# Lower-threshold compare of every second weight piece on GpSimd, in the first ternary feed-forward block

## Chip, cores and metric

One core of one Trainium2 chip. The metric is the device time of the whole kernel in microseconds, lower is better. Engine names are those of the profile: PE is TensorE's matmuls, PEld its weight loads, DVE is VectorE, ACT is ScalarE, POOL is GpSimd, SP is SyncE, which here issues the DMAs.

## What is computed

A macaron layer on x of 4 x 512 tokens by 512 features: half of a feed-forward block, a recurrent attention block, and half of the same feed-forward block again. The change is in the first feed-forward block:

```python
def _quantize(w):
    gamma = jnp.mean(jnp.abs(w))
    return jnp.clip(jnp.round(w / (gamma + EPS)), -1.0, 1.0)

def _bitlinear(x, w):
    return jnp.matmul(x, _quantize(w).T)
x1 = _bitlinear(x, w1)      # w1, w2: 1408 x 512
x2 = _bitlinear(x, w2)
hidden = jax.nn.sigmoid(x1) * x2
return _bitlinear(hidden, w3)   # w3: 512 x 1408

x = x + 0.5 * _L0_ffn_ref(_layernorm(x, axis=-1), L0_ffn_w1, L0_ffn_w2, L0_ffn_w3)
```

A quantised weight is 1 where w is above half of gamma, -1 where it is below minus half of gamma, and 0 between: two comparisons and a subtraction.

## The kernel before, in words

The kernel has three phases, one after the other: `ffn_phase` with `first=True`, the attention, and `ffn_phase` with `first=False`. The first phase quantises the three weights and saves them; the last one loads them. Each engine runs its own list of instructions in the order in which it is written, and waits on semaphores where it needs another's result.

In the first phase, each weight lies in SBUF as 128 partitions by 5632 float32 values, cut into four pieces (k = 0 to 3) of 1408. SP loads the tokens and then the twelve pieces. ACT sums the absolute values of each piece as it lands (L208). PE adds them over the partitions (`total`, L326), and DVE makes the two thresholds `thr` and `nthr` of weight i (`threshold`, L257 to L264). Then `quantise(i)` goes over the four pieces on DVE, two instructions for each:

```python
dve.wait_ge(quantised, KT * i + k)
nc.vector.tensor_scalar(below[:, :], raw[i][:, piece], nthr[:, i:i + 1], None, ALU.is_lt).then_inc(below_ready, 1)
dve.wait_ge(below_ready, KT * i + k + 1)
nc.vector.scalar_tensor_tensor(wq[i][:, piece], raw[i][:, piece], thr[:, i:i + 1],
                               below[:, :], ALU.is_gt, ALU.subtract).then_inc(quantised, 1)
```

The first (L273) writes "below the lower threshold" as bfloat16 into `below`; the second (L276), called the quantising instruction here, compares the piece with the upper threshold and subtracts `below`. There is one buffer `below`, so DVE goes through compare, quantise, compare, quantise, twelve times in all. For w3, `raw[2]` is a part of `x_sb`.

DVE's list in this phase is: norm of the first 512 tokens, their split, threshold and quantise of w1, of w2, of w3, then `hidden(0, 0)` (L284 to L291), which multiplies the two up projections and splits the product into `g_hi` and `g_lo`. PE's list is: transposes, the totals of w1 and w2, the first two row tiles of the w1 product (as each piece is quantised), the total of w3, the same two tiles of w2, then `down_tile(0, 0)` (L379), which needs `g_lo` of `hidden(0, 0)`. From there on PE alternates up tiles and down tiles. SP waits until all twelve pieces are quantised before it loads the other token rows into `x_sb` and saves `wq`. POOL has little to do: the constants, and for each block b of 512 tokens two small instructions on a 128 x 4 tile that make `rstd` (L193, L195), those for b = 1 when DVE has the statistics of the second 512 tokens.

Of the kernel before, what the change touches and what calls it, by code (L numbers as in the profile page):

```python
# [25 lines left out]
BF16 = mybir.dt.bfloat16  # L26
# [4 lines left out]
P = 128  # L31
NB, T, HID = 4, 512, 512
NH = 16
FF = 1408
C = T // P
KT = HID // P
# [10 lines left out]
def ffn_phase(nc, first, x_in, x_out, w_t, wq_dram):  # L47

    with ExitStack() as ctx:  # L49
        def sb(name, shape, dt=FP32):  # L50
            return ctx.enter_context(nc.sbuf_tensor(f"{name}_{int(first)}", shape, dt))

        def sem(name):
            return ctx.enter_context(nc.semaphore(f"{name}_{int(first)}"))
# [18 lines left out]
        hid = sb("hid", [P, 2, T])  # L73
        g_hi = [sb(f"g_hi{i}", [P, T], F32R) for i in range(2)]
        g_lo = [sb(f"g_lo{i}", [P, T], F32R) for i in range(2)]
        if first:
            raw = [sb(f"raw{i}", [P, KT * FF])[:, :] for i in range(2)]
            raw.append(x_sb[:, C:, :].rearrange("p c d -> p (c d)")[:, 0:KT * FF])
            below = sb("below", [P, FF], BF16)
            junk = sb("junk", [P, 3 * HID], BF16)  # L80
            asum = sb("asum", [P, 3, KT])
            tot = sb("tot", [P, 3])
            gamma = sb("gamma", [P, 3])
            thr = sb("thr", [P, 3])
            nthr = sb("nthr", [P, 3])
# [6 lines left out]
        abs_summed = sem("abs_summed")  # L92
        total_ready = sem("total_ready")
        thr_step = sem("thr_step")
        below_ready = sem("below_ready")
        quantised = sem("quantised")
        wq_saved = sem("wq_saved")
        groups = [(m, min(m + 3, MT)) for m in range(0, MT, 3)]
# [83 lines left out]
        @block.gpsimd  # L182
        def _(pool):
            nc.gpsimd.memset(ident[:, :], 0.0).then_inc(consts_ready, 1)
            nc.gpsimd.memset(ones[:, :], 1.0).then_inc(consts_ready, 1)
            nc.gpsimd.memset(eps_t[:, :], LN_EPS).then_inc(consts_ready, 1)
            nc.gpsimd.memset(mhalf[:, :], -0.5).then_inc(consts_ready, 1)
            pool.wait_ge(consts_ready, 4)
            nc.gpsimd.affine_select(out=ident[:, :], in_=ident[:, :], compare_op=ALU.not_equal, fill=1.0, base=0,
                                    pattern=[[-1, P]], channel_multiplier=1).then_inc(consts_ready, 1)  # L190
            for b in range(NB):
                pool.wait_ge(stats_step, 2 * C * (b + 1))
                nc.gpsimd.tensor_tensor(ve[:, :], mv[:, :, 1], eps_t[:, :], ALU.add).then_inc(rstd_step, 1)  # L193
                pool.wait_ge(rstd_step, 2 * b + 1)
                nc.gpsimd.tensor_tensor(rstd[:, :], ve[:, :], mhalf[:, :], ALU.pow).then_inc(rstd_step, 1)  # L195
# [24 lines left out]
        @block.vector  # L220
        def _(dve):
            def x_rows(b, c):
                return x_sb[:, b * C + c, :]

            def norm_stats(b):

                dve.wait_ge(x_full[b], 16)
                nc.vector.memset(gate[:, :], 0.0)
                for c in range(C):
                    nc.vector.bn_stats(stats[:, c, :], x_rows(b, c)).then_inc(stats_step, 1)  # L230
                dve.wait_ge(stats_step, 2 * C * b + C)
                nc.vector.memset(gate[:, :], 0.0)
                for c in range(C):
                    nc.vector.bn_aggr(mv[:, c, :], stats[:, c, :]).then_inc(stats_step, 1)  # L234

            def norm_apply(b):
                dve.wait_ge(rstd_step, 2 * b + 2)
                dve.wait_ge(ln_transposed, KT * b)
                for c in range(C):
                    nc.vector.tensor_scalar(xn[:, c, :], x_rows(b, c), mv[:, c, 0:1], rstd[:, c:c + 1],  # L240
                                            ALU.subtract, ALU.mult).then_inc(xn_ready, 1)

            def split_norm(b, half):

                for k in (2 * half, 2 * half + 1):
                    bank = up_ps[k % 2][pair["rows", b, half]]
                    dve.wait_ge(ln_transposed, KT * b + k + 1)
                    nc.vector.tensor_copy(h_hi[b % 2][:, k, :], bank[:, :]).then_inc(h_split, 1)  # L248
                    dve.wait_ge(h_split, 2 * (KT * b + k) + 1)
                    nc.vector.tensor_tensor(h_lo[b % 2][:, k, :], bank[:, :], h_hi[b % 2][:, k, :].bitcast(FP32),  # L250
                                            ALU.subtract).then_inc(h_split, 1)

            def threshold(i):

                s = 4 * i
                dve.wait_ge(total_ready, i + 1)
                nc.vector.tensor_reduce(tot[:, i:i + 1], out_ps[i][:, 0:KT], AX.X, ALU.add).then_inc(thr_step, 1)  # L257
                dve.wait_ge(thr_step, s + 1)
                nc.vector.tensor_scalar(gamma[:, i:i + 1], tot[:, i:i + 1], 1.0 / (FF * HID), Q_EPS,
                                        ALU.mult, ALU.add).then_inc(thr_step, 1)  # L260
                dve.wait_ge(thr_step, s + 2)
                nc.vector.tensor_scalar(nthr[:, i:i + 1], gamma[:, i:i + 1], -0.5, None,
                                        ALU.mult).then_inc(thr_step, 1)
                nc.vector.tensor_scalar(thr[:, i:i + 1], gamma[:, i:i + 1], 0.5, None,  # L264
                                        ALU.mult).then_inc(thr_step, 1)
                dve.wait_ge(thr_step, s + 4)

            def quantise(i):

                for k in range(KT):  # L270
                    piece = slice(k * FF, (k + 1) * FF)
                    dve.wait_ge(quantised, KT * i + k)
                    nc.vector.tensor_scalar(below[:, :], raw[i][:, piece], nthr[:, i:i + 1], None,  # L273
                                            ALU.is_lt).then_inc(below_ready, 1)
                    dve.wait_ge(below_ready, KT * i + k + 1)
                    nc.vector.scalar_tensor_tensor(wq[i][:, piece], raw[i][:, piece], thr[:, i:i + 1],  # L276
                                                   below[:, :], ALU.is_gt, ALU.subtract).then_inc(quantised, 1)

            def hidden(b, m):

                n = MT * b + m
                dve.wait_ge(sig_ready, n + 1)
                dve.wait_ge(value_in, n + 1)
                nc.vector.tensor_tensor(hid[:, n % 2, :], up_ps[1][pair["tile", b, m]][:, :], sig[:, n % 2, :],  # L284
                                        ALU.mult).then_inc(hid_step, 1)
                dve.wait_ge(hid_step, 3 * n + 1)
                if n >= 2:
                    dve.wait_ge(down_done, n - 1)
                nc.vector.tensor_copy(g_hi[n % 2][:, :], hid[:, n % 2, :]).then_inc(hid_step, 1)  # L289
                dve.wait_ge(hid_step, 3 * n + 2)  # L290
                nc.vector.tensor_tensor(g_lo[n % 2][:, :], hid[:, n % 2, :], g_hi[n % 2][:, :].bitcast(FP32),  # L291
                                        ALU.subtract).then_inc(hid_step, 1)

            def add_output(b):
                dve.wait_ge(down_done, MT * (b + 1))
                for c in range(C):
                    nc.vector.scalar_tensor_tensor(x_rows(b, c), out_ps[c][:, :], 0.5, x_rows(b, c),  # L297
                                                   ALU.mult, ALU.add).then_inc(out_added, 1)

            norm_stats(0)  # L300
            norm_apply(0)
            split_norm(0, 0)
            split_norm(0, 1)
            if first:
                for i in range(3):
                    threshold(i)
                    quantise(i)
            for b in range(NB):
                for m in range(MT):
                    hidden(b, m)  # L310
                    if m == 0 and b > 0:
                        add_output(b - 1)
                    if b + 1 < NB:
                        if m == MT - 7:
                            norm_stats(b + 1)
                        if m == MT - 6:
                            norm_apply(b + 1)
                        if m >= MT - 4 and m < MT - 2:
                            split_norm(b + 1, m - (MT - 4))
            add_output(NB - 1)  # L320
# [1214 lines left out]
```

## Time and profile before

| | us |
|---|---|
| time, median of 3 runs | 3064.88 (3059.52 to 3068.61) |
| the profiled execution | 3062.89 |
| its span in the trace | 3061.2 |
| busy in the span: PE, DVE, ACT, POOL | 2937.7, 2183.8, 1625.3, 1349.5 |

The span is the time from the first instruction of the program to the last, and the execution's own time lies 1.7 us over it. Busy time is the time in which an engine had an instruction of the program under way. The first feed-forward phase takes about the first tenth of the span, the attention about eight tenths.

### The profile page before, as it was taken

What the parts mean: (1) busy time and instruction counts of PE and PEld (TensorE: products, weight loads), DVE (VectorE), ACT (ScalarE), POOL (GpSimd) and SP (SyncE); (2) the same over time, 40 slices, a digit from 0 to 9 for tenths busy, and PEclk for the clock granted to TensorE, in tenths of its full rate; (3) what the DMA queues carried; (4) which work ended last, traced back from release to release, by engine and by line L of the source; (5) the groups of instructions that cost most, each with busy time, mean ns of one, the idle gap of its engine ahead of it and who ended that gap; (6) DMA issues with size and microseconds to landing.
All of it is one profiled execution on the core that took longest, in us unless ns stands there. A gap on an engine that the chain in (4) does not pass through costs nothing. (4 is left out here: it accounts for less than half of the span.)

```text
span 3061.2 us, 44753 instructions
## 1 busy us (share of the span) xinstructions
PE 2937.7 (96%) x14918; PEld 2068.1 (68%) x14918; DVE 2183.8 (71%) x4724; ACT 1625.3 (53%) x3682; POOL 1349.5 (44%) x1999
## 2 busy tenths in 40 slices
PE   5999699999999999999999999999999999996999
PEld 4887466666666666666666666666666666664887
DVE  6553488787785887877868777777678777773553
ACT  3110376666665666666656666666666666660110
POOL 0000465555554555555545555555455555550000
PEclk8999899999999999999999999999999999998999
DMA  6100311111111111111011111110111111105000
GB/s 242 54 14 20 108 37 35 32 47 32 46 32 58 49 56 33 46 32 49 28 62 48 55 32 46 35 45 28 48 49 52 32 49 32 46 27 182 14 14 28
DMA packets 89638, 151.15 MB, mean 49 GB/s; under 512 B 9152, under 2 KB 30784, under 8 KB 89024
## 3 DMA queue, kind: packets, MB, share of 16 engines
q1 hardware_dynamic: 89408, 148.29, 15.1%
q8 instruction: 120, 1.97, 0.3%
q14 instruction: 110, 0.90, 0.1%
HBM read 127.02 MB, written 21.23 MB: 48 GB/s over the span
## 5 line engine op out<-in xcount | busy, mean ns | idle before, releaser
L714 POOL TENSOR_TENSOR Y<-aT,D 128x256 f32<-128x256 f32 x384 | 274.5, 751 | 495.8 <-ACT aT L907 495.8
L714 POOL TENSOR_TENSOR s<-s,tmp 128x256 f32<-128x256 f32 (+1 forms) x448 | 353.8, 790 | 292.2 <-DVE tmp L970 255.0
L714 POOL TENSOR_TENSOR X<-S,D 128x256 f32<-128x256 f32 x384 | 288.5, 751 | 176.8 <-ACT S L867 88.5
L217 ACT ACTIVATE sig<-up_ps 128x512 f32<-128x512 f32 x88 | 52.7, 599 | 473.1 <-PE up_ps L356 473.0
L356 PE MATMUL up_ps<-h_hi,wq 128*128 128x512 f32 x704 | 284.2, 404 | 9.9 <-DVE wq L276 8.6
L356 PE MATMUL up_ps<-h_lo,wq 128*128 128x512 f32 x704 | 280.7, 399 | 0.0
L1276 PE MATMUL ps<-hT,slot_k 128*128 128x512 f32 x512 | 264.0, 602 | 1.3 <-ACT beta L826 1.3
L1276 PE MATMUL ps<-hT,slot_q 128*128 128x512 f32 x512 | 261.8, 593 | 0.0
L1276 PE MATMUL ps<-hT,slot_v 128*128 128x512 f32 x512 | 261.7, 594 | 0.0
L1276 PE MATMUL ps<-hT,slot_w 128*128 128x512 f32 x512 | 260.3, 593 | 0.0
L1297 PEld LDWEIGHTS ps<-AM,XT 128*128 128x128 f32 x1536 | 206.5, 192 | 58.6 <-issue 42.9
L1051 DVE COPY_PREDICATED A<-mask,ps 128x256 f32<-128x256 int32 x448 | 236.5, 528 | 10.7 <-DVE A L1051 0.7
L1243 PE MATMUL ps<-wo,og 128*128 128x512 f32 x512 | 242.8, 600 | 1.1 <-DVE og L1187 1.1
L1305 PEld LDWEIGHTS ps<-Y,S 128*128 128x128 f32 x1536 | 201.3, 192 | 62.7 <-issue 58.7
L970 DVE TENSOR_TENSOR tmp<-ps,D 128x256 f32<-128x256 f32 (+1 forms) x448 | 190.6, 438 | 70.7 <-PE ps L1348 47.0
L284 DVE TENSOR_TENSOR hid<-up_ps,sig 128x512 f32<-128x512 f32 x88 | 60.9, 693 | 250.1 <-PE up_ps L356 250.1
L1297 PE MATMUL ps<-AM,XT 128*128 128x128 f32 x1536 | 224.3, 276 | 0.7 <-DVE AM L970 0.7
L1305 PE MATMUL ps<-Y,S 128*128 128x128 f32 x1536 | 213.3, 275 | 1.1 <-DVE A L1051 1.1
L1024 DVE SCALAR_TENSOR_TENSOR acc_w<-ps,tap,acc_w 128x511 f32<-128x511 f32 (+2 forms) x192 | 143.8, 749 | 86.5 <-ACT acc_w L844 82.0
L970 DVE TENSOR_TENSOR D<-D 128x256 f32<-128x256 f32 x384 | 185.1, 482 | 16.2 <-ACT D L861 1.9
L970 DVE TENSOR_TENSOR AM<-As,mask 128x256 f32<-128x256 f32 x448 | 189.5, 446 | 0.0
L1243 PEld LDWEIGHTS ps<-wo,og 128*128 128x128 f32 x512 | 98.6, 193 | 124.8 <-issue 124.8
(187 smaller groups left out, 6882.9 us busy)
## 6 DMA issues: line engine op xcount, KB each, us to landing
slot_k<-in_wk_dram SPq DMA_DIRECT2D x64, 256.0 KB, 2.6
slot_w<-in_ww_dram SPq DMA_DIRECT2D x64, 256.0 KB, 2.6
slot_q<-in_wq_dram SPq DMA_DIRECT2D x64, 256.0 KB, 2.6
slot_v<-in_wv_dram SPq DMA_DIRECT2D x64, 256.0 KB, 2.6
wo<-in_wo_dram SPq DMA_DIRECT2D x64, 256.0 KB, 3.8
wq_dram<-wq SPq DMA_DIRECT2D x3, 2816.0 KB, 24.0
wq<-wq_dram SPq DMA_DIRECT2D x9, 768.0 KB, 12.1
raw<-in_w_dram SPq DMA_DIRECT2D x8, 704.0 KB, 10.7
```

The lines of the kernel that those rows point to most:

```text
L217: nc.scalar.activation(sig[:, n % 2, :], up_ps[0][pair["tile", b, m]][:, :], ACT.Sigmoid).then_inc(sig_ready, 1)
L284: nc.vector.tensor_tensor(hid[:, n % 2, :], up_ps[1][pair["tile", b, m]][:, :], sig[:, n % 2, :], ALU.mult).then_inc(hid_step, 1)
L356: last = nc.tensor.matmul(up_ps[which][pair["tile", b, m]][:, :], up[which][:, k, m * P:(m + 1) * P], part[b % 2][:, k, :], start=(k == 0 ...
L714: return nc.gpsimd.tensor_tensor(out, in0, in1, op)
L970: return nc.vector.tensor_tensor(out, in0, in1, op)
L1024: nc.vector.scalar_tensor_tensor(acc[x][:, j:], bank[x][:, 0:T - j], tap[:, at:at + 1], acc[x][:, j:], ALU.mult, ALU.add).then_inc(dve_ear ...
L1051: nc.vector.copy_predicated(targets(A2, l), by_target(mask[l], l).bitcast(INT32), by_target(bank[f"a2_{l}"], l)).then_inc(dve_late, 1)
L1243: mm = nc.tensor.matmul(into[:, :], ck_(og[:, (C * group + j) % (2 * C), :], c), wo[j][:, :], start=(j == 0), stop=(j == C - 1))
L1276: mm = nc.tensor.matmul(bank[x][:, :], ck_(slot[x], kk), hT[:, kk, :], start=(kk == 0), stop=(kk == KT - 1))
L1297: last = nc.tensor.matmul(pair_columns(bank[f"s{l}"], i), XT[l][:, i, :], pair_columns(AM[l], i), start=True, stop=True)
L1305: last = nc.tensor.matmul(pair_columns(bank[f"a2_{l}"], i), ck_(S[l], i), odd_targets(aT, i) if l == 1 else pair_columns(Y[l], i), start=T ...
```

## The change

POOL makes the lower comparison of the odd pieces (k = 1 and 3) of each weight, in a buffer of its own; DVE keeps that of the even ones. The second buffer is a bfloat16 view of `hid`, which is not in use before `hidden(0, 0)`. POOL's comparison of an odd piece waits for the thresholds of its weight and, from the second on, until DVE has quantised the odd piece before it, which is when the buffer is free (for k = 1 of w2 and w3 this is piece 3 of the weight before; for k = 3 it is piece 1). The quantising instruction of an odd piece waits for POOL's semaphore. `hidden(0, 0)` gets a wait for all twelve pieces.

```diff
-            below = sb("below", [P, FF], BF16)
+            below = [sb("below", [P, FF], BF16)[:, :], hid[:, :, :].rearrange("p a t -> p (a t)").bitcast(BF16)[:, 0:FF]]
...
-        below_ready = sem("below_ready")
+        below_even = sem("below_even")
+        below_odd = sem("below_odd")
...
+            def below_threshold(i, k):
+
+                pool.wait_ge(thr_step, 4 * i + 4)
+                if KT * i + k >= 2:
+                    pool.wait_ge(quantised, KT * i + k - 1)
+                nc.gpsimd.tensor_scalar(below[1], raw[i][:, k * FF:(k + 1) * FF], nthr[:, i:i + 1], None,
+                                        ALU.is_lt).then_inc(below_odd, 1)
+
             for b in range(NB):
+                if first and b == 1:
+                    for i in range(3):
+                        for k in range(1, KT, 2):
+                            below_threshold(i, k)
                 pool.wait_ge(stats_step, 2 * C * (b + 1))
...
                 for k in range(KT):
                     piece = slice(k * FF, (k + 1) * FF)
-                    dve.wait_ge(quantised, KT * i + k)
-                    nc.vector.tensor_scalar(below[:, :], raw[i][:, piece], nthr[:, i:i + 1], None,
-                                            ALU.is_lt).then_inc(below_ready, 1)
-                    dve.wait_ge(below_ready, KT * i + k + 1)
+                    if k % 2 == 0:
+                        dve.wait_ge(quantised, KT * i + k)
+                        nc.vector.tensor_scalar(below[0], raw[i][:, piece], nthr[:, i:i + 1], None,
+                                                ALU.is_lt).then_inc(below_even, 1)
+                        dve.wait_ge(below_even, KT // 2 * i + k // 2 + 1)
+                    else:
+                        dve.wait_ge(below_odd, KT // 2 * i + k // 2 + 1)
                     nc.vector.scalar_tensor_tensor(wq[i][:, piece], raw[i][:, piece], thr[:, i:i + 1],
-                                                   below[:, :], ALU.is_gt, ALU.subtract).then_inc(quantised, 1)
+                                                   below[k % 2], ALU.is_gt, ALU.subtract).then_inc(quantised, 1)
...
                 dve.wait_ge(value_in, n + 1)
+                if first and n == 0:
+                    dve.wait_ge(quantised, 3 * KT)
```

On POOL, in the first phase, between the `rstd` instructions of the first and of the second 512 tokens. The last rows of its list before:

```order
L189 AFFINE_SELECT ident<-ident 128x128
L193 TENSOR_TENSOR ve<-mv,eps_t 128x4
L195 TENSOR_TENSOR rstd<-ve,mhalf 128x4
L193 TENSOR_TENSOR ve<-mv,eps_t 128x4
L195 TENSOR_TENSOR rstd<-ve,mhalf 128x4
```

and now, where `hid` is the view that holds the comparison and `x_sb` the raw w3:

```order
L190 AFFINE_SELECT ident<-ident 128x128
L206 TENSOR_TENSOR ve<-mv,eps_t 128x4
L208 TENSOR_TENSOR rstd<-ve,mhalf 128x4
L197 TENSOR_SCALAR hid<-raw_1,nthr 128x1408 x4
L197 TENSOR_SCALAR hid<-x_sb,nthr 128x1408 x2
L206 TENSOR_TENSOR ve<-mv,eps_t 128x4
L208 TENSOR_TENSOR rstd<-ve,mhalf 128x4
```

Six comparisons stand there that were not on POOL before; the `rstd` pair of the second 512 tokens is behind them. On DVE, the four pieces of w1 before:

```order
L264 TENSOR_SCALAR thr<-gamma 128x1
L273 TENSOR_SCALAR below<-raw_1,nthr 128x1408
L276 SCALAR_TENSOR_TENSOR wq_1<-raw_1,thr,below 128x1408
L273 TENSOR_SCALAR below<-raw_1,nthr 128x1408
L276 SCALAR_TENSOR_TENSOR wq_1<-raw_1,thr,below 128x1408
L273 TENSOR_SCALAR below<-raw_1,nthr 128x1408
L276 SCALAR_TENSOR_TENSOR wq_1<-raw_1,thr,below 128x1408
L273 TENSOR_SCALAR below<-raw_1,nthr 128x1408
L276 SCALAR_TENSOR_TENSOR wq_1<-raw_1,thr,below 128x1408
```

and now:

```order
L277 TENSOR_SCALAR thr<-gamma 128x1
L287 TENSOR_SCALAR below<-raw_1,nthr 128x1408
L292 SCALAR_TENSOR_TENSOR wq_1<-raw_1,thr,below 128x1408
L292 SCALAR_TENSOR_TENSOR wq_1<-raw_1,thr,hid 128x1408
L287 TENSOR_SCALAR below<-raw_1,nthr 128x1408
L292 SCALAR_TENSOR_TENSOR wq_1<-raw_1,thr,below 128x1408
L292 SCALAR_TENSOR_TENSOR wq_1<-raw_1,thr,hid 128x1408
```

The comparisons of pieces 1 and 3 are gone, and the quantising instruction of an odd piece follows that of the even one.

## Rows read from the trace of the kernel before

**Rows 1.** The page: span and busy time of each engine.

```profile
span 3061.2 us, 44753 instructions
...
PE 2937.7 (96%) x14918; PEld 2068.1 (68%) x14918; DVE 2183.8 (71%) x4724; ACT 1625.3 (53%) x3682; POOL 1349.5 (44%) x1999
```

**Rows 2.** Timeline of DVE, 8 to 31 us: start us, duration us, engine, line, operation.

```profile
8.89 0.28 DVE L234 BATCH_NORM_AGGREGATE mv<-stats 128x2 f32<-128x6 f32 x3
...
19.52 0.14 DVE L264 TENSOR_SCALAR thr<-gamma 128x1 f32<-128x1 f32 x1
19.70 0.95 DVE L273 TENSOR_SCALAR below<-raw,nthr 128x1408 bf16<-128x1408 f32 x1
20.69 1.69 DVE L276 SCALAR_TENSOR_TENSOR wq<-raw,thr,below 128x1408 fp32r<-128x1408 f32 x1
22.41 0.95 DVE L273 TENSOR_SCALAR below<-raw,nthr 128x1408 bf16<-128x1408 f32 x1
```

**Rows 3.** Timeline of DVE, 50 to 56 us.

```profile
51.50 1.68 DVE L276 SCALAR_TENSOR_TENSOR wq<-x_sb,thr,below 128x1408 fp32r<-128x1408 f32 x1
53.10 0.69 DVE L284 TENSOR_TENSOR hid<-up_ps,sig 128x512 f32<-128x512 f32 x1
...
54.29 0.69 DVE L291 TENSOR_TENSOR g_lo<-hid,g_hi 128x512 fp32r<-128x512 f32 x1
```

**Rows 4.** Timeline of PE, 45 to 56 us.

```profile
45.55 0.40 PE L356 MATMUL up_ps<-h_lo,wq 128*128 128x512 f32 x1
55.03 0.79 PE L379 MATMUL out_ps<-wq,g_hi 128*128 128x512 f32 x1 [9.09 <-DVE g_lo L291]
```

**Rows 5.** Windows: us, then busy us of PE, PEld, DVE, ACT, POOL.

```profile
19.70:53.10 33.40, 15.46 (x36) 9.58 (x36) 32.44 (x32) 10.06 (x15) 0.00 (x0) 0.83 0.22 81
55.00:310.00 255.00, 246.27 (x1072) 198.56 (x1072) 117.31 (x211) 25.14 (x42) 4.25 (x12) 0.98 0.16 63
```

**Rows 6.** Tile below: duration ns min/median/max, first and last start.

```profile
L273 DVE TENSOR_SCALAR below<-raw,nthr x8: 953/953/954, 19.7 to 39.2; 128x1408 bf16<-128x1408 f32 x8
```

**Rows 7.** Groups of POOL by shape: busy us, mean ns of one.

```profile
L714 POOL TENSOR_TENSOR s<-s,tmp 128x384 f32<-128x384 f32 x64 | 63.7, 996 | 13.2 <-DVE tmp L970 12.6
...
L714 POOL TENSOR_TENSOR r<-r,rs 128x4 f32<-128x4 f32 x64 | 12.9, 201 | 5.0
...
L699 POOL MEMSET mask<- 128x256 f32 x7 | 1.8, 311 | 0.0
...
L189 POOL TENSOR_SCALAR_AFFINE_SELECT ident<-ident 128x128 f32<-128x128 f32 x2 | 0.6, 292 | 0.4 <-POOL mhalf L187 0.2
L184 POOL MEMSET ident<- 128x128 f32 x2 | 0.4, 204 | 22.1 <-POOLq L515 21.8 <-POOLq L1525 0.3
```

**Rows 8.** Line L714, one of its forms: duration ns min/median/max.

```profile
L714 POOL TENSOR_TENSOR X<-S,D x384: 619/723/1101, 354.6 to 2730.0; 128x256 f32<-128x256 f32 x192
```

**Rows 9.** Timeline, 637.8 to 638.5 us, DVE and POOL.

```profile
637.91 0.43 DVE L970 TENSOR_TENSOR D<-D 128x256 f32<-128x256 f32 x1
637.95 1.10 POOL L714 TENSOR_TENSOR X<-S,D 128x256 f32<-128x256 f32 x1 [0.60 <-ACT S L867]
```

**Rows 10.** Timeline, 640.1 to 640.6 us, POOL and DVE.

```profile
639.96 0.74 POOL L714 TENSOR_TENSOR X<-S,D 128x256 f32<-128x256 f32 x1
640.20 0.79 DVE L970 TENSOR_TENSOR D<-D 128x256 f32<-128x256 f32 x1
```

**Rows 11.** Groups of DVE by shape: one of the attention phase, one of L240.

```profile
L970 DVE TENSOR_TENSOR D<-u_g 128x256 f32<-128x256 f32 x64 | 26.9, 420 | 0.0
...
L240 DVE TENSOR_SCALAR xn<-x_sb,mv,rstd 128x512 f32<-128x512 f32 x32 | 15.3, 543 | 2.8 <-POOL rstd L195 2.8
```

**Rows 12.** Lines L985 and L1081: duration ns min/median/max.

```profile
L985 DVE TENSOR_SCALAR xn_a<-xn_a,mv_a,rstd_a x16: 533/950/2023, 318.6 to 2110.2; 128x512 f32<-128x512 f32 x16
L1081 DVE TENSOR_SCALAR tap<-per_head x64: 215/858/1097, 324.4 to 2705.6; 128x13 f32<-128x13 f32 x64
```

**Rows 13.** Timeline of POOL, 0 to 120 us.

```profile
9.25 0.20 POOL L193 TENSOR_TENSOR ve<-mv,eps_t 128x4 f32<-128x4 f32 x1 [7.51 <-DVE mv L234]
...
78.65 0.20 POOL L193 TENSOR_TENSOR ve<-mv,eps_t 128x4 f32<-128x4 f32 x1 [68.10 <-DVE mv L234]
```

## The prediction

> **What bounds the kernel now.** The page comes first: over the whole span PE is busy 96% of the time, DVE 71% and POOL 44% [rows 1]. That average does not say what the change is worth, because the change acts in one stage of some 33 us near the start, and there the order is another. The timeline of DVE shows the stage. From 19.70 us on DVE does compare (0.95 us), quantise (1.69 us), compare, and so on: one piece starts 2.71 us after the other (22.41 - 19.70) and the gap between instructions is 0.03 to 0.04 us [rows 2]. Twelve pieces later, at 53.10 us, it reaches `hidden(0, 0)` [rows 3]. The window of that stretch confirms that DVE has no slack: 32.44 us busy of 33.40, while PE has 15.46 and POOL nothing [rows 5]. PE is the one that waits. Its first down tile starts at 55.03 us, after an idle time of 9.09 us that ended with DVE's `g_lo` [rows 4], and this `g_lo` is the third instruction behind the last piece on DVE [rows 3]. From 55 to 310 us, to the end of the phase and into the turn to the attention, PE is busy 246.27 us of 255 [rows 5]. So the end of the quantising chain moves all that comes later by its own shift. A microsecond won or lost between 19.70 and 53.10 us is a microsecond of the kernel, and nothing behind it takes it up.
>
> **The change, part by part.** The unit of the sum is a pair of pieces, an even one and an odd one; there are six pairs. A pair takes 2 x 2.71 = 5.42 us before [rows 2].
>
> Removed from DVE: six comparisons, each 953 ns [rows 6], which with its gap is 0.99 us of the chain (20.69 - 19.70) [rows 2].
>
> Added on POOL: six comparisons of 128 x 1408. POOL has no such instruction in the trace. Call the duration of one T and bound it by POOL's rows [rows 7]. At the low end, a memset reads nothing: 204 ns for 128 columns and 311 ns for 256 are 0.84 ns a column and about 0.10 us fixed, which gives T = 1.27 us. At the high end stands an operation with two tensors in: 201 ns for 4 columns and 996 ns for 384 are 2.09 ns a column, which gives T = 3.13 us. Nearest to the new instruction is the affine select, since it reads one tensor, compares and writes one: 292 ns for 128 columns, less 0.10 us fixed, are 1.50 ns a column, so T = 0.10 + 1408 x 1.50 = 2.21 us. I take this one; it is an extrapolation over eleven times the columns.
>
> Do both engines work at once? If they do, T of 2.21 us is hidden: POOL starts at the thresholds or at the end of the odd piece before, as DVE's own comparison does, and DVE needs the result only 0.95 + 0.04 + 1.68 = 2.67 us later. But the rows of the attention phase speak against it. At 637.91 us DVE runs `D<-D`, whose two inputs are both in SBUF; POOL's `X<-S,D` has started 0.04 us later and lasts 1.10 us [rows 9], against a least duration of 0.62 and a median of 0.72 us for this line [rows 8]. It ends 0.71 us after DVE's instruction did (639.05 against 638.34), as if it had started only then. The other way round, POOL is at work from 639.96 to 640.70 us, and a `D<-D` that starts at 640.20 us takes 0.79 us and ends at 640.99 [rows 10], where one of the same size has a mean of 420 ns [rows 11]: all but 0.29 us of it lies behind POOL's end. A DVE `tensor_scalar` with one tensor in behaves alike. On 512 columns it takes 543 ns at L240, where POOL is idle [rows 11], but a median of 950 ns and up to 2023 at L985; and the one on 13 columns at L1081 takes between 215 and 1097 ns with a median of 858, beside POOL's work [rows 12]. Both instructions of `quantise` are of these kinds: the comparison is a `tensor_scalar` from SBUF to SBUF, and the quantising one has `raw` and `below` in SBUF. So I reckon that POOL's comparison and DVE's two instructions exclude each other.
>
> The Trainium skill, "SBUF — State Buffer", section on who interferes with whom, has this as a rule: a Vector instruction in a two-port mode, or with two SBUF inputs against a GpSimd instruction that reads, takes the shared port pair for its whole length and the other one blocks fully. The rows just read agree; by the opposite view, with no lock, the sum would be that of the first rival below.
>
> With exclusion, a pair goes like this. Thresholds ready (or the odd piece before quantised), DVE starts its comparison within 0.04 us (19.66 to 19.70) [rows 2], POOL wakes 0.08 us after a DVE result (9.17 [rows 2] to 9.25 [rows 13]) and is held. DVE's comparison ends after 0.95 us. In the 0.04 us that DVE needs before its quantising instruction, POOL gets in and runs for T; that it costs the full T I take from the 0.71 us in rows 9. DVE's quantising instruction ends 1.68 - 0.13 us after POOL, 0.13 being the difference between 0.42 and 0.29 us in rows 10. The second one follows with 0.03 us gap and 1.68 us, and 0.03 us on the next pair begins. Sum: 0.95 + T + 1.55 + 0.03 + 1.68 + 0.03 = 4.24 + T, against 5.42 us. The difference is T - 1.18 us a pair. Should DVE win the race for the 0.04 us, or POOL start first, the same pieces stand in another order with the same sum but for a wake-up of 0.08 us. With T = 2.21 us that is +1.03 us a pair and **+6.2 us** for six. The bounds are +0.5 us (T = 1.27) and +11.7 us (T = 3.13).
>
> Other edits go together at nothing. `hidden(0, 0)`'s new wait is for what DVE itself has just done. Behind POOL's six comparisons stands the `rstd` pair of the second 512 tokens, which is due at 78.65 us [rows 13]; the comparisons end before DVE's last piece, so by about 57 us at most. SP's loads and saves start when the twelfth piece is done, as before, and shift with the chain. PE's w1 and w2 tiles shift with the pieces and end well before `g_lo` (45.95 against 54.98 us [rows 3, 4]). If DVE's part became shorter by more than these 9 us, PE's tiles would be late next; nothing here comes near it.
>
> The profiled execution took 3062.89 us, 1.7 us over its span [rows 1]; with 6.2 us more it is 3069.1 us. The median of the runs lies 2.0 us above the profiled one, so the forecast as a median is 3064.9 + 6.2 = **3071 us**.
>
> **The rivals.** Bound for all: a measurement of this kernel can tell about 0.3%, 9.2 us, from no change; most cases here lie inside.
>
> *They overlap after all.* Then a pair is 0.95 + 0.04 + 1.68 + 0.03 + 1.68 + 0.03 = 4.41 us, 1.01 us less, and six are -6.1 us: 3058.8 us. For it: POOL is idle in the stage and T of 2.21 us fits under 2.67. The instructions of rows 9 to 12 are not the ones of the change. Against it: those rows show exclusion in both directions and for both kinds of DVE instruction. Even the full gain stays under 9.2 us, so this case is faster but within 0.3%. Chance 0.12.
>
> *POOL is as fast as its memset, and the engines exclude each other.* T = 1.27 us, +0.5 us: 3065.4 us. For it: each column may cost POOL one step whatever it does. Against: affine select and two-input operations are slower by column [rows 7]. Chance 0.25. The Trainium skill, "GPSIMD Engine Reference", section on engine selection, says that one-input operations there run at roughly line rate, which is this case; no row shows a one-input arithmetic operation on POOL.
>
> *POOL is as slow as with two tensors, and the place where it tells is the same hold.* T = 3.13 us gives +11.7 us: 3076.6 us, slower by 0.38%. It decides from T = 1.18 + 9.2 / 6 = 2.71 us on, that is at 1.86 ns a column; the extrapolated 1.50 ns needs to be off by a quarter. For it: a scalar read per partition, a type change to bfloat16, and a hold beyond the sum per pair all add. Against: the nearest row. Chance 0.15.
>
> *The forecast*, exclusion with T between about 1.6 and 2.7 us, has the other 0.48.
>
> **How the numbers follow.** 3071 us is the forecast. The range reaches from the case of overlap to that of a slow POOL with some scatter of a median on top: 3059 to 3079 us. Faster by over 0.3% would need 9.2 us, more than all six comparisons (6 x 0.99 = 5.9 us) with their gaps give; 0.02 is for scatter between the runs, which reach from 3059.5 to 3068.6 us. Slower by over 0.3%: the slow case's 0.15 and the upper edge of the forecast, 0.18. Within: 0.80.
>
> **What would show it.** In the profile of the changed kernel, the time from DVE's first comparison to `hidden(0, 0)` should be 33.40 + 6.2 = 39.6 us; 27.3 means overlap. The quantising instruction of the even pieces should be recorded long, about T + 1.5 us, and those of the odd pieces 1.68 us; DVE's comparisons stay at 0.95 us. POOL's comparison is recorded as T plus the time that it is held, some 3.1 us. The idle time of PE before its first down tile should grow. With exclusion refuted, even and odd ones are all at 1.68 us. The prediction is wrong as a whole if the chain does not pass on its shift: if `hidden(0, 0)` starts late and the down tiles of the last tokens do not.

## The result and the profile after

The changed kernel takes 3072.88 us (median of 6 runs, 3070.67 to 3077.3), the kernel before 3064.1 us (6 runs, 3059.52 to 3068.61). The ratio is 1.003 with a 95% interval from 1.0017 to 1.0043: slower by 8.8 us, or 0.3%, where 3071 us had been forecast.

The page of the changed kernel, first lines:

```profile
span 3070.5 us, 44758 instructions
## 1 busy us (share of the span) xinstructions
PE 2937.9 (96%) x14918; PEld 2066.7 (67%) x14918; DVE 2190.8 (71%) x4718; ACT 1626.3 (53%) x3682; POOL 1378.2 (45%) x2005
```

DVE has six instructions fewer than before (4718 against 4724) and is busy 7 us longer, 2190.8 against 2183.8 us [rows 1]. POOL has six more and 28.7 us more. The timeline of DVE, 19 to 34 and 56 to 66 us (start us, duration us, engine, line, operation), shows where DVE's time went:

```profile
19.72 0.95 DVE L287 TENSOR_SCALAR below<-raw,nthr 128x1408 bf16<-128x1408 f32 x1
20.71 4.49 DVE L292 SCALAR_TENSOR_TENSOR wq<-raw,thr,below 128x1408 fp32r<-128x1408 f32 x1
25.13 1.67 DVE L292 SCALAR_TENSOR_TENSOR wq<-raw,thr,hid 128x1408 fp32r<-128x1408 f32 x1
26.83 0.95 DVE L287 TENSOR_SCALAR below<-raw,nthr 128x1408 bf16<-128x1408 f32 x1
...
63.46 0.69 DVE L302 TENSOR_TENSOR hid<-up_ps,sig 128x512 f32<-128x512 f32 x1
...
64.64 0.69 DVE L309 TENSOR_TENSOR g_lo<-hid,g_hi 128x512 fp32r<-128x512 f32 x1
```

and that of POOL, 0 to 120 us:

```profile
19.79 4.60 POOL L197 TENSOR_SCALAR hid<-raw,nthr 128x1408 bf16<-128x1408 f32 x1 [9.20 <-DVE thr L277]
26.97 4.52 POOL L197 TENSOR_SCALAR hid<-raw,nthr 128x1408 bf16<-128x1408 f32 x1 [2.58 <-DVE wq L292]
...
88.73 0.20 POOL L206 TENSOR_TENSOR ve<-mv,eps_t 128x4 f32<-128x4 f32 x1 [27.81 <-DVE mv L247]
```

DVE's comparison takes 0.95 us as before. The quantising instruction of the even piece is recorded at 4.49 us where it took 1.69 [rows 2], and the 2.8 us more are called the hold here; that of the odd piece has its old length. A pair takes 26.83 - 19.72 = 7.11 us against 5.42. `hidden(0, 0)` starts at 63.46 us instead of 53.10 [rows 3]. The stretch from the first comparison to it is 43.7 us instead of 33.4, 10.3 us longer. PE passes this on:

```profile
65.39 0.80 PE L397 MATMUL out_ps<-wq,g_hi 128*128 128x512 f32 x1 [12.89 <-DVE g_lo L309]
```

Its first down tile starts 10.36 us later than before, after 12.89 us of idleness instead of 9.09 [rows 4]; the rest of the delay lies in PE's waits for the quantised pieces ahead of it. In the windows of the stretch and of the 255 us behind it (columns as in rows 5),

```profile
19.70:62.00 42.30, 15.66 (x36) 9.55 (x36) 41.75 (x26) 10.06 (x15) 27.36 (x6) 0.79 0.18 65
63.00:318.00 255.00, 245.98 (x1072) 197.99 (x1072) 119.42 (x215) 25.16 (x42) 3.67 (x6) 0.98 0.16 63
```

DVE is "busy" for 41.75 of 42.30 us, but some 17 us of that are the hold of six instructions, and the stage behind is the old one (245.98 us of PE against 246.27 [rows 5]).

Six times the 2.8 us by which the even quantising instruction grew would be 17 us. Against that, six comparisons of 0.99 us left the chain, and the second quantising instruction starts 0.07 us before the end of the first (25.13 against 25.20) where a comparison used to follow after a gap of 0.03 us. Together that gives the 10.3 us, within 0.1 us.

### The profile page after: what moved, and what is told of

The parts are those of the page before. It is cut to its first block and busy times, and to the rows that moved or that the text cites. A ratio compares the mean times of both kernels' runs of the same rounds, so it can differ in the third digit from the quotient of the medians.

```text
span 3070.5 us, 44758 instructions
## 1 busy us (share of the span) xinstructions
PE 2937.9 (96%) x14918; PEld 2066.7 (67%) x14918; DVE 2190.8 (71%) x4718; ACT 1626.3 (53%) x3682; POOL 1378.2 (45%) x2005
## 3 DMA queue, kind: packets, MB, share of 16 engines
q8 instruction: 120, 1.97, 0.3%
```

## The experiments

Three things had to be told apart: whether the two engines really keep each other out or only slow each other down; which operand of DVE's instruction does it; and why the hold is 2.8 us. All kernels here but the one with six pieces on ACT were executed once, so I read their traces rather than their times. Names as in the changed kernel; line numbers differ a little.

### POOL first

```diff
                         dve.wait_ge(quantised, KT * i + k)
+                        dve.wait_ge(below_odd, KT // 2 * i + k // 2 + 1)
                         nc.vector.tensor_scalar(below[0], raw[i][:, piece], nthr[:, i:i + 1], None,
```

> DVE's comparison of the even piece also waits for POOL's comparison of the odd one, so POOL runs with DVE idle and then DVE with POOL idle. Exclusion theory (POOL was held until DVE's comparison ended at 20.67 us, then needed 3.72 us): POOL's comparison is recorded at 3.7 us, all DVE instructions at their old 0.95 and 1.68 us, a pair of pieces takes 0.08 + 3.7 + 0.08 + 0.95 + 0.04 + 1.68 + 0.03 + 1.68 + 0.03 = 8.3 us, and the stretch from the first comparison to hidden(0, 0) is about 51 us. Rival, POOL simply needs 4.5 us and DVE's comparison never held it: recorded 4.5 us, a pair 9.1 us. Rival, both engines share a bandwidth and slow each other down: POOL alone is clearly under 3.7 us.

Timeline of this run, POOL and then DVE:

```profile
19.83 3.84 POOL L197 TENSOR_SCALAR hid<-raw,nthr 128x1408 bf16<-128x1408 f32 x1 [9.21 <-DVE thr L277]
28.24 3.83 POOL L197 TENSOR_SCALAR hid<-raw,nthr 128x1408 bf16<-128x1408 f32 x1 [4.57 <-DVE wq L293]
```

```profile
23.80 0.95 DVE L288 TENSOR_SCALAR below<-raw,nthr 128x1408 bf16<-128x1408 f32 x1 [4.08 <-POOL hid L197]
24.79 1.68 DVE L293 SCALAR_TENSOR_TENSOR wq<-raw,thr,below 128x1408 fp32r<-128x1408 f32 x1
...
71.03 0.69 DVE L303 TENSOR_TENSOR hid<-up_ps,sig 128x512 f32<-128x512 f32 x1
```

POOL alone needs 3.84 us. The pair, from one POOL start to the next, takes 8.41 us (28.24 - 19.83), and `hidden(0, 0)` starts at 71.03 us, 51.2 us after POOL's first comparison, which now opens the stretch. The exclusion theory said 3.7, 8.3 and 51. In the changed kernel POOL's 4.60 us end 3.72 us after the end of DVE's comparison (24.39 - 20.67), and the 4.52 us of the second one 3.71 us (31.49 - 27.78), though POOL had started only 0.07 and 0.14 us after that comparison did. So POOL had been held until the comparison ended. The rival of 4.5 us and that of a shared bandwidth, where POOL alone would have been faster than 3.7, fall.

### POOL late

```diff
-                pool.wait_ge(thr_step, 4 * i + 4)
+                pool.wait_ge(below_even, KT // 2 * i + k // 2 + 1)
```

> POOL's comparison waits for DVE's comparison of the even piece instead of the thresholds, so it is released about 0.08 us after that ends, 0.04 us after DVE has begun to quantise. Exclusion theory (whoever comes first keeps the other out): the even quantising instruction is back at 1.68 us, POOL is held behind it and recorded at 1.6 + 3.7 = 5.3 us, and the odd quantising waits for POOL's end: a pair is 0.95 + 0.04 + 1.68 + 3.7 + 0.08 + 1.68 + 0.03 = 8.2 us. Rival, shared bandwidth: order does not matter, even quantising stays near 4.5 us and a pair near the 7.1 us of the changed kernel.

```profile
19.87 0.95 DVE L287 TENSOR_SCALAR below<-raw,nthr 128x1408 bf16<-128x1408 f32 x1
20.86 1.69 DVE L292 SCALAR_TENSOR_TENSOR wq<-raw,thr,below 128x1408 fp32r<-128x1408 f32 x1
20.92 5.33 POOL L197 TENSOR_SCALAR hid<-raw,nthr 128x1408 bf16<-128x1408 f32 x1 [10.21 <-DVE below L287]
26.28 1.69 DVE L292 SCALAR_TENSOR_TENSOR wq<-raw,thr,hid 128x1408 fp32r<-128x1408 f32 x1 [3.74 <-POOL hid L197]
28.00 0.95 DVE L287 TENSOR_SCALAR below<-raw,nthr 128x1408 bf16<-128x1408 f32 x1
```

These are lines of the timeline of both engines. POOL wakes 0.06 us after DVE has begun to quantise, and now it is DVE that keeps its 1.69 us and POOL that is held: its record grows to 5.33 us, and it ends 3.70 us after DVE's instruction. A pair takes 8.13 us, against 8.2 expected. Who comes first decides who waits; a shared bandwidth would not mind the order. In the changed kernel it was POOL that came first at this point: it had been standing there since 19.79 us, so it could go on at the end of DVE's comparison (20.67 us), 0.04 us before DVE's next instruction (20.71 us).

### The second input from PSUM

The even quantising instruction reads zeros from PSUM in place of `below`, so the even pieces lose their -1; the work of both engines is otherwise the same.

```diff
-                    nc.vector.scalar_tensor_tensor(wq[i][:, piece], raw[i][:, piece], thr[:, i:i + 1],
-                                                   below[k % 2], ALU.is_gt, ALU.subtract).then_inc(quantised, 1)
+                    if k % 2 == 0:
+                        second = out_ps[3][:, 0:quarter].rearrange("p (o n) -> p o n", o=1).to_broadcast([P, 4, quarter])
...
+                                                       thr[:, i:i + 1], second, ALU.is_gt,
```

> The quantising instruction of the even pieces takes its second input from PSUM (352 zeros read four times over) instead of the buffer below, so the lower comparison of even pieces is made but not used and their weights lack the -1. Exclusion through the second SBUF input: this instruction is recorded at about 1.7 us beside a running POOL, POOL stays at 4.5 to 4.6 us, and a pair is 0.95 + 3.72 + 0.08 + 1.67 + 0.03 = 6.45 us instead of 7.1. Rival, POOL keeps any DVE instruction out, or any traffic in SBUF slows: it stays near 4.5 us and a pair near 7.1 us.

Timeline of DVE, then the first row of POOL:

```profile
20.27 0.95 DVE L287 TENSOR_SCALAR below<-raw,nthr 128x1408 bf16<-128x1408 f32 x1
21.27 1.68 DVE L295 SCALAR_TENSOR_TENSOR wq<-raw,thr,out_ps 128x1408 fp32r<-128x1408 f32 x1
24.97 1.68 DVE L300 SCALAR_TENSOR_TENSOR wq<-raw,thr,hid 128x1408 fp32r<-128x1408 f32 x1 [2.03 <-POOL hid L197]
26.69 0.95 DVE L287 TENSOR_SCALAR below<-raw,nthr 128x1408 bf16<-128x1408 f32 x1
...
59.86 0.69 DVE L310 TENSOR_TENSOR hid<-up_ps,sig 128x512 f32<-128x512 f32 x1
```

```profile
20.34 4.60 POOL L197 TENSOR_SCALAR hid<-raw,nthr 128x1408 bf16<-128x1408 f32 x1 [9.80 <-DVE thr L277]
```

With one input in SBUF and the other in PSUM, the even quantising instruction takes 1.68 us in the middle of POOL's work, and POOL takes the 4.60 us that it took. A pair takes 6.42 us (26.69 - 20.27) against 6.45 expected, and the stretch is 39.6 us (20.27 to 59.86). So it is through its second input in SBUF that DVE's instruction was held. Yet the stretch is still 6.2 us over that of the kernel before: with the hold gone, DVE waits 2.03 us for POOL's result. Of these, 0.76 us (4.60 for the 3.84 us alone) are POOL's own wait behind DVE's comparison, and the other 1.27 us are POOL's slowness. Whether a second buffer for POOL, so that it can work a piece ahead, would hide that wait was not tried.

### What a POOL comparison costs by itself

Six POOL instructions at the start of the kernel, one after the other, while DVE waits for the last of them; their input is constants.

```diff
+                probes = [lambda: nc.gpsimd.tensor_scalar(below[1], src, nthr[:, 0:1], None, ALU.is_lt),
+                          lambda: nc.gpsimd.tensor_scalar(below[1][:, 0:half], src[:, 0:half], nthr[:, 0:1], None, ALU.is_lt),
...
+                          lambda: nc.gpsimd.tensor_copy(wide, src[:, 0:half])]
```

> Six GpSimd instructions by themselves at the start, while VectorE is held back (the kernel is longer by their sum, some 15 to 20 us): the comparison of the change on 1408 columns and on 704, then on 704 columns the same with a float32 result, a multiplication by the same per-partition scalar, the comparison with an immediate, and a copy. Exclusion theory: 1408 columns take 3.8 us as in the run where POOL goes first, 704 columns about 1.95 us, so 2.6 ns a column, a two-input rate. Rival for the slow rate: the bfloat16 result or the per-partition scalar costs it, then one of the other forms is clearly faster (about 1.2 us at 1.5 ns a column).

```profile
3.11 3.84 POOL L200 TENSOR_SCALAR hid<-xn,nthr 128x1408 bf16<-128x1408 f32 x1
7.05 2.04 POOL L201 TENSOR_SCALAR hid<-xn,nthr 128x704 bf16<-128x704 f32 x1
9.18 2.04 POOL L202 TENSOR_SCALAR sig<-xn,nthr 128x704 f32<-128x704 f32 x1
11.32 2.06 POOL L203 TENSOR_SCALAR sig<-xn,nthr 128x704 f32<-128x704 f32 x1
13.46 1.97 POOL L204 TENSOR_SCALAR sig<-xn 128x704 f32<-128x704 f32 x1
15.50 0.77 POOL L205 COPY sig<-xn 128x704 f32<-128x704 f32 x1
```

Expected were 3.8 us for 1408 columns and 1.95 us for 704. In the order of the timeline: the comparison at 1408 and at 704 columns, with a float32 result, the multiplication (L203), the comparison with an immediate (L204), the copy. From 2.04 to 3.84 us over 704 columns are 2.56 ns a column and 0.24 us fixed. Neither the bfloat16 result nor the per-partition scalar (0.07 us) nor the comparison makes it slow: all four forms of `tensor_scalar` on 704 columns take 1.97 to 2.06 us, and only the copy takes 0.77 us. DVE makes the same comparison in 0.95 us, a quarter of POOL's time.

### Fewer columns on POOL

The change with 704, 352 or 1056 columns of each odd piece on POOL. The other columns are not compared at all, by DVE either; a memset of POOL's buffer ahead of the stage leaves zeros there.

```diff
-                nc.gpsimd.tensor_scalar(below[1], raw[i][:, k * FF:(k + 1) * FF], nthr[:, i:i + 1], None,
+                nc.gpsimd.tensor_scalar(below[1][:, 0:part], raw[i][:, k * FF:k * FF + part], nthr[:, i:i + 1], None,
```

> POOL compares 704 of the 1408 columns of each odd piece; the other half is not compared with the lower threshold (its weights lack the -1). If the cost per pair is 4.24 us plus POOL's exclusive time, 2.87 us in the changed kernel and by columns, then it falls to about 1.5 us and a pair to 5.7 us against 5.42 before: the stretch is about 35 us and the kernel within 2 us of the kernel before. Rival, the cost is a fixed price of going over to POOL and back: a pair stays near 7 us.

> POOL compares 352 of 1408 columns of each odd piece; the other columns are not compared with the lower threshold (their weights lack the -1). POOL alone needs 0.24 + 352 x 2.56 ns = 1.14 us. Measured so far: DVE's quantising instruction is kept out for 2.85 us after its comparison at 1408 columns and for 0.51 us at 704, although POOL runs on for 0.87 and 1.42 us. Theory, DVE gets in once POOL has taken its input in, which runs ahead of the arithmetic by some hundred columns: at 352 columns nothing is held, the even quantising instruction is recorded at 1.68 us and the stretch is about 27.7 us. Rival, each GpSimd comparison holds a fixed time at least: recorded 2.1 us, as with 704 columns.

> POOL compares 1056 of 1408 columns; the rest is left out as before. POOL alone: 2.94 us. If the hold grows evenly with the columns, it is half-way between 0.51 and 2.85 us, 1.7 us, and the even quantising instruction is recorded at 3.3 us. Rival, the input is taken in large steps: it is near 2.1 us, as at 704 columns, or near 4.5 us, as at 1408.

The first POOL instruction and the even quantising one beside it, from the timelines of the runs with 704,

```profile
19.87 2.81 POOL L198 TENSOR_SCALAR hid<-raw,nthr 128x704 bf16<-128x704 f32 x1 [9.22 <-DVE thr L278]
20.79 2.15 DVE L293 SCALAR_TENSOR_TENSOR wq<-raw,thr,below 128x1408 fp32r<-128x1408 f32 x1
```

with 352,

```profile
19.79 1.92 POOL L198 TENSOR_SCALAR hid<-raw,nthr 128x352 bf16<-128x352 f32 x1 [9.21 <-DVE thr L278]
20.71 1.86 DVE L293 SCALAR_TENSOR_TENSOR wq<-raw,thr,below 128x1408 fp32r<-128x1408 f32 x1
```

and with 1056 columns:

```profile
19.89 3.72 POOL L198 TENSOR_SCALAR hid<-raw,nthr 128x1056 bf16<-128x1056 f32 x1 [9.21 <-DVE thr L278]
20.82 2.45 DVE L293 SCALAR_TENSOR_TENSOR wq<-raw,thr,below 128x1408 fp32r<-128x1408 f32 x1
23.65 1.69 DVE L293 SCALAR_TENSOR_TENSOR wq<-raw,thr,hid 128x1408 fp32r<-128x1408 f32 x1 [0.38 <-POOL hid L198]
```

| columns on POOL | even quantising, us | over 1.68, us | stretch, us |
|---|---|---|---|
| 352 | 1.86 | 0.18 | 47.71 - 19.72 = 28.0 |
| 704 | 2.15 | 0.47 | 49.57 - 19.80 = 29.8 |
| 1056 | 2.45 | 0.77 | 54.12 - 19.83 = 34.3 |
| 1408 | 4.49 | 2.81 | 63.46 - 19.72 = 43.7 |

My expectation for 704 columns was wrong: I had said a hold of about 1.5 us and a stretch of 35, from 2.87 us in proportion. The one for 352 was nearly right (28.0 us against 27.7, but 0.18 us of hold instead of none). For 1056 neither 3.3 us nor the nearest step holds. Up to there the hold grows by 0.84 ns a column (0.59 us over 704 columns), the rate of POOL's memset [rows 7], and is far shorter than POOL's work. DVE gets in long before POOL is done: with 704 columns POOL runs on until 22.68 us and takes 1.93 us from the end of DVE's comparison, hardly other than the 2.04 us alone. From 1056 to 1408 columns the hold grows by 2.04 us, 5.8 ns a column. That the first part is the time in which POOL takes its input in, ahead of its arithmetic, would fit its rate, but it is my reading and no run shows it; nor can the records tell a DVE instruction that starts late from one that runs slower. Why the last quarter costs so much, no run here settles.

The short stretches are no gain yet, since work is left out of them. With 704 columns on POOL the stretch is 3.6 us under that of the kernel before (33.4 - 29.8). If DVE made the other half of each comparison in half of 0.95 us and a gap of 0.04, six of them would take 3.1 us; by this estimate half a microsecond would be left. It was not tried.

### One comparison in two instructions

Nothing is left out here: POOL compares both halves, and DVE's odd quantising instruction waits for the second.

```diff
+                for at in (0, half):
+                    nc.gpsimd.tensor_scalar(below[1][:, at:at + half], raw[i][:, k * FF + at:k * FF + at + half],
+                                            nthr[:, i:i + 1], None, ALU.is_lt).then_inc(below_odd, 1)
```

> POOL makes each comparison in two instructions of 704 columns (nothing is left out). The even quantising instruction should get in after the first one's input, 0.51 us, and be recorded at 2.15 us; the second POOL instruction is then held until it ends and needs 1.93 us more, and the odd quantising instruction waits for it: a pair takes about 6.7 us and the stretch about 41.5 us, against 43.7 for the changed kernel and 33.4 before. Rival, POOL goes from one instruction to the next without letting DVE in: recorded 4.4 us or more and the stretch 44 us.

```profile
19.72 0.95 DVE L289 TENSOR_SCALAR below<-raw,nthr 128x1408 bf16<-128x1408 f32 x1
20.71 2.15 DVE L294 SCALAR_TENSOR_TENSOR wq<-raw,thr,below 128x1408 fp32r<-128x1408 f32 x1
24.80 1.69 DVE L294 SCALAR_TENSOR_TENSOR wq<-raw,thr,hid 128x1408 fp32r<-128x1408 f32 x1 [1.94 <-POOL hid L199]
26.52 0.95 DVE L289 TENSOR_SCALAR below<-raw,nthr 128x1408 bf16<-128x1408 f32 x1
```

The even quantising instruction takes 2.15 us, as expected, and a pair 6.80 us against 6.7; the stretch is 41.95 us (61.67 - 19.72), 1.8 us under the changed kernel and still 8.5 us over the one before. The hold shrinks from 2.8 to 0.5 us, and its place is taken by 1.94 us of waiting for POOL's second half.

### The comparison on ACT

From the kernel before, with pieces 1, 2 and 3 of w2 and w3 compared by ACT, which after 29.2 us has only a table load and two sigmoids of 0.60 us left in this stretch. DVE makes one more small number for each weight, `kthr = -0.5 * STEEP * gamma`, and the steep sigmoid gives 0 or 1. A sigmoid on one column ahead of the comparisons brings the table load forward, to 29.27 us from 31.85. These are as many pieces as the change moves, but other ones; the run with pieces 1 and 3 of w2 and w3 moves four that the change moves too.

```diff
+STEEP = float(2 ** 40)
...
+                for at, (i, k) in enumerate(on_act):
+                    act.wait_ge(thr_step, 5 * i + 5)
...
+                    nc.scalar.activation(spare[at % 2], raw[i][:, k * FF:(k + 1) * FF],
+                                         ACT.Sigmoid, scale=-STEEP, bias=kthr[:, i:i + 1]).then_inc(below_act, 1)
```

> From the kernel before: pieces 1, 2 and 3 of w2 and w3 get their lower comparison from ACT (a sigmoid of 2^40 times the distance below the threshold, which is 0 or 1), in the view of hid and in the buffer of the absolute sums in turn; DVE keeps the comparison of the other six pieces. If what costs in the change is that POOL and DVE exclude each other, ACT's 1.4 us lie beside DVE's 1.68 us and cost nothing: quantising instructions stay at 1.68 us, six comparisons of 0.99 us leave the chain, two small threshold instructions of 0.08 us come in, and the kernel is 5.8 us faster than before, about 3059 us (0.19%). Rival, SBUF traffic of any second engine slows DVE: quantising is recorded above 1.8 us and the kernel is no faster.

> As the run with six pieces on ACT, but pieces 1 and 3 of w2 and w3 alone: four comparisons less on DVE, as many pieces as the change moves for these two weights. No exclusion: the stretch from the first comparison to hidden(0, 0) is 33.4 - 4 x 0.99 + 0.16 = 29.6 us. Rival: 33 us or more.

> The same kernel as the run with six pieces on ACT, again. Its stretch was 27.2 us against 33.4, 6.2 us less, but its median 13 us under that of the kernel before. If the rest was scatter of the attention phase, the median is now 6 us under it (ratio 0.998); if it belongs to the kernel, again some 13 us (0.9955).

Timeline of DVE in the run with six pieces, and of ACT beside it:

```profile
31.29 0.95 DVE L296 TENSOR_SCALAR below<-raw,nthr 128x1408 bf16<-128x1408 f32 x1
32.28 1.68 DVE L300 SCALAR_TENSOR_TENSOR wq<-raw,thr,below 128x1408 fp32r<-128x1408 f32 x1
33.88 1.68 DVE L300 SCALAR_TENSOR_TENSOR wq<-raw,thr,hid 128x1408 fp32r<-128x1408 f32 x1
...
47.13 0.69 DVE L310 TENSOR_TENSOR hid<-up_ps,sig 128x512 f32<-128x512 f32 x1
```

```profile
31.35 1.47 ACT L225 ACTIVATE hid<-raw,kthr 128x1408 bf16<-128x1408 f32 x1 [0.58 <-DVE kthr L282]
32.73 1.45 ACT L225 ACTIVATE junk<-raw,kthr 128x1408 bf16<-128x1408 f32 x1
```

ACT reads `raw` and writes its result at the same time as DVE's comparison and its quantising instruction, and DVE's two keep the 0.95 and 1.68 us that they take without it. ACT's comparison takes 1.45 to 1.47 us whichever of them it stands beside; it was not timed alone. The first three quantising instructions of a weight follow each other every 1.60 us. The stretch is 27.3 us (47.13 - 19.88), 6.2 us less than before where 5.8 were expected; with four pieces on ACT it is 29.3 us, against 29.6 expected. So a second engine beside DVE does not cost as such; it is POOL that does.

The six-piece kernel has a median of 3050.86 us (5 runs) beside 3063.86 us, ratio 0.9953 (0.9939 to 0.9966), and in a second set 3059.5 us (9 runs) beside 3066.17 us, ratio 0.9976 (0.9966 to 0.9986). Both intervals lie under 1, so it is faster than the kernel before, by 0.2 to 0.5%; the changed kernel is slower than that one by 0.3%. The 6.2 us of the stretch explain the 6.7 us of the second set. The 13 us of the first stay open: its trace is of an execution of 3059.55 us, and the other four took 3050.05 to 3051.02 us and have none.

### How far the stretch carries to the end

The attention phase adds some scatter of its own. In the kernel before, its first ACT instruction starts at 325.81 us and the last feed-forward phase has its first sigmoid at 2803.91, 2478.1 us later; in the changed kernel:

```profile
335.72 0.60 ACT L828 ACTIVATE hT<-ps 128x512 f32<-128x512 f32 x1 [29.58 <-PE ps L1230]
...
2813.20 0.60 ACT L230 ACTIVATE sig<-up_ps 128x512 f32<-128x512 f32 x1 [18.20 <-PE up_ps L374]
```

that is 2477.5 us. With POOL late it is 2474.1 us, with the input from PSUM 2481.7. So the time of a single execution differs by some microseconds from what its stretch says, and I judge mechanisms by the stretch alone.

## Why the prediction was right, and what was off in it

*Bound and pass-through.* Right. The stretch grew by 10.3 us, PE's first down tile came 10.36 us later, the attention started 9.9 us later (335.72 against 325.81) and the span grew by 9.3 us (3070.5 against 3061.2); the medians differ by 8.8 us. PE's 246 us in the next 255 are unchanged. The microsecond that is missing at the end is within the scatter between executions.

*Exclusion.* Right in who waits for whom, wrong in how long. That POOL is held by DVE's comparison shows in its end 3.72 us after it, and that it is held by DVE's quantising instruction in the 3.70 us of the run with POOL late. That POOL holds DVE's quantising instruction is shown by the 4.49 us beside POOL against 1.68 us in the run with POOL first, and that it does so through the second input in SBUF by the run with that input from PSUM. That POOL holds a DVE comparison, which the prediction took from rows 12, is tested by no run here, since no comparison of this stage starts beside a working POOL. The rules of the Trainium skill that bear on it ("SBUF — State Buffer", who interferes with whom) agree here in who waits and which operands count, but not in "fully blocks": if DVE's instruction needs its 1.68 us at the end of its record, it was let in 0.87 us before POOL's end, and 1.42 and 2.02 us before it with 704 and 1056 columns. The first rival, overlap (27.3 us), fell. One reading of the prediction is turned round: of the 0.79 us of `D<-D` in rows 10, 0.29 us lie behind POOL's end (640.99 - 640.70), not all but 0.29; the 0.13 us drawn from it in the sum use it the right way.

*T*, the duration of POOL's comparison, is the term that was mis-sized. I took 2.21 us at 1.50 ns a column from the affine select, with 3.13 us as the high end. It is 3.84 us alone, 2.56 ns a column, above the bound: a `tensor_scalar` on POOL is slower by column than its two-tensor multiplication, at 2.09 ns [rows 7]. So the second rival, T of 1.27 us, fell too. The line rate that the Trainium skill gives for one-input operations ("GPSIMD Engine Reference", engine selection) is not seen for any `tensor_scalar` here, only the copy (0.77 us for 704 columns) comes near the memset's 0.84 ns a column. A warning stood in the trace of the kernel before: other affine selects of the same 128 x 128 take from 0.31 to 1.31 us, so the one of 0.29 us was no safe measure by column. Line L705 there, duration ns min/median/max:

```profile
L705 POOL TENSOR_SCALAR_AFFINE_SELECT mask<-mask x14: 310/406/1307, 320.5 to 335.5; 128x128 f32<-128x128 f32 x14
```

*The handover.* I let POOL exclude DVE for the whole of T, less 0.13 us. It does so for less: with 1408 columns DVE's instruction ends 0.81 us after POOL's (25.20 - 24.39), so 0.87 of its 1.68 us lie beside POOL, instead of 0.13.

*The sum.* Per pair, in the prediction's terms: +1.03 us forecast, +1.63 for T (3.84 for 2.21), -0.74 for the handover (0.87 for 0.13), -0.12 because POOL ended 3.72 us after DVE's comparison and not 3.84, and -0.10 for two quantising instructions that overlap by 0.07 us instead of having a gap of 0.03. That makes +1.70; measured, 7.11 - 5.42 = +1.69. Six pairs are 10.2 us against a forecast of 6.2. So the stretch was missed by 4.1 us (39.6 forecast, 43.7 measured), although the errors in T and in the handover partly cancel. That the time was missed by 1.9 us only (3071 against 3072.88) is luck on top: the executions of one kernel scatter by several microseconds. By its size the outcome is that of the third rival, a POOL slow enough: its point was an exclusive T of 2.71 us, and the exclusive part, in the sense of 4.24 + T = 7.11, is 2.87.

*Edits at nothing.* Right: the `rstd` pair of the second 512 tokens starts at 88.73 us, long after POOL's last comparison, and follows DVE's statistics, not POOL.

## What to carry to other kernels

Before work is moved from DVE to POOL, look in the trace whether the two work at the same time at all. A DVE instruction with two inputs in SBUF that is short when POOL idles and recorded long beside POOL's work says that they do not, and then POOL's instruction counts in DVE's chain. Even where they do overlap, POOL's comparison took four times as long as DVE's here, so there must be that much slack. Here ACT was the better place: it made the same comparison in 1.47 us and lengthened none of DVE's instructions, at the price of one small DVE instruction for each weight.

## What the runs showed of the hardware that I had not expected

A GpSimd `tensor_scalar` (3.84 us for 1408 columns) is slower than DVE's by four and, by column, than GpSimd's own two-tensor multiplication (2.56 against 2.09 ns [rows 7]), while a copy of 704 columns takes 0.77 us. And the time by which it lengthens a DVE instruction with two SBUF inputs is not its duration: 0.18, 0.47 and 0.77 us for 352, 704 and 1056 columns, then 2.81 us for 1408.
